# A decoder layer: cross-attention's k and v projected during self-attention and passed through DRAM

## The reference

```python
# self-attention, per batch and head (D = 32)
scores = (q @ k.T + rel_q + rel_k) / sqrt(D)     # rel_q[l, r] = q[l] . dist_emb[l - r + 511]
ctx = softmax(scores) @ v                        # rel_k[l, r] = k[r] . dist_emb[l - r + 511]
x = layernorm(x + layernorm(ctx @ Wo + bo + x))
# cross-attention, per batch and head (64 wide); c is the second input
q, k, v = x @ Wq + bq, c @ Wk + bk, c @ Wv + bv
x = layernorm(x + (softmax(causal(q @ k.T / 8)) @ v) @ Wo + bo)
# slots, 16 experts, and attention from the tokens to the slots
x = layernorm(x + slot_mixture(x))
```

## Time and profile before

| what | value |
|---|---|
| median of 3 runs | 4272.65 us (4272.12 to 4275.99) |
| the profiled execution, its own time | 4274.03 us |
| its span, first to last instruction | 4272.1 us |
| mean granted TensorE clock | 0.942 of full |
| busy share: TensorE, VectorE, ScalarE, POOL | 86%, 52%, 39%, 44% |
| bytes moved by DMA | 1151.74 MB |
| self-attention | about 50 to 1695 us |
| its projection and norms | to about 1945 us |
| cross-attention | about 1945 to 3107 us |

### The profile page before, as it was taken

The page is one execution under the profiler, slowest core; times in us unless marked ns, Lnnn a source line. Parts: engine busy times, 40 slices in busy tenths (PEclk is TensorE's granted clock), DMA queues, the critical chain, the costliest instruction groups (busy, mean ns, idle before and its releaser), DMA issues. The chain is left out here.

```text
span 4272.1 us, 67667 instructions
## 1 busy us (share of the span) xinstructions
PE 3681.4 (86%) x19584; PEld 2298.4 (54%) x19584; DVE 2230.7 (52%) x6128; ACT 1678.6 (39%) x3639; POOL 1859.8 (44%) x1684
## 2 busy tenths in 40 slices
PE   6988888888888886769999999999989987788686
PEld 4766666667676674325556666655545552122244
DVE  4666676767666665773554555455523231111155
ACT  4666666666666664333333333333312110000023
POOL 3766666667676665433444444444511100000012
PEclk9999999999999998989999999999989998898798
DMA  6999999999999997455555555555355328999723
GB/s 246 399 375 391 386 385 374 386 369 386 373 388 377 385 387 295 142 176 194 180 180 175 173 172 176 179 178 180 128 183 186 107 74 350 420 421 421 290 79 118
DMA packets 544321, 1151.74 MB, mean 270 GB/s; under 512 B 34240, under 2 KB 206912, under 8 KB 494912
## 3 DMA queue, kind: packets, MB, share of 16 engines
q1 hardware_dynamic: 539520, 1141.13, 71.7%
q10 hardware_dynamic: 4032, 7.34, 0.5%
q0 software_dynamic: 512, 0.26, 0.0%
HBM read 745.46 MB, written 403.18 MB: 269 GB/s over the span
## 5 line engine op out<-in xcount | busy, mean ns | idle before, releaser
L433 POOL TENSOR_SCALAR a_sc<-a_sc,a_inv 128x512 f32<-128x512 f32 x512 | 818.5, 1602 | 383.1 <-DVE a_inv L383 313.1
L1004 POOL TENSOR_SCALAR b_sc<-b_sc,b_inv 128x128 f32<-128x128 f32 (+3 forms) x512 | 549.6, 1082 | 657.5 <-DVE b_inv L957 657.5
L284 ACT ACTIVATE a_stage_q<-a_ps_q 128x640 f32<-128x640 f32 x512 | 360.0, 703 | 469.8 <-PE a_ps_q L201 442.5
L962 DVE COPY b_pt<-b_ps_t 128x128 f32<-128x128 f32 (+3 forms) x512 | 250.2, 489 | 547.3 <-PE b_ps_t L863 547.3
L390 DVE COPY a_pt<-a_ps_t 128x512 f32<-128x512 f32 x512 | 353.6, 691 | 280.3 <-PE a_ps_t L187 242.3
L376 DVE CUSTOM_DVE_ANT_0 a_sc<-a_ps_s,a_rq 128x512 f32<-128x512 f32 x512 | 353.9, 691 | 197.2 <-PE a_ps_s L177 145.0
L918 ACT ACTIVATE b_sc<-b_sc,b_mx 128x128 f32<-128x128 f32 (+3 forms) x512 | 281.0, 550 | 446.7 <-DVE b_mx L951 446.7
L274 ACT ACTIVATE a_sc<-a_sc,a_mx 128x512 f32<-128x512 f32 x512 | 370.5, 724 | 77.5 <-DVE a_mx L376 75.9
L175 PE MATMUL a_ps_s<-a_ks,a_qs 128*128 128x512 f32 x512 | 261.2, 510 | 139.4 <-DMA a_rk<-band_k 103.9
L284 ACT ACTIVATE a_stage_k<-a_ps_k 128x640 f32<-128x640 f32 x512 | 359.1, 701 | 30.4 <-DMA band_k<-a_stage_k 30.4
L187 PEld LDWEIGHTS a_ps_t<-a_ident,a_sc 128*128 128x128 f32 x2048 | 249.9, 145 | 218.2 <-issue 201.2
(11 more groups left out here) (200 smaller groups left out, 6159.5 us busy)
## 6 DMA issues: line engine op xcount, KB each, us to landing
band_q<-a_stage_q SPq DMA_DIRECT2D x128, 1280.0 KB, 9.0
band_k<-a_stage_k SPq DMA_DIRECT2D x128, 1280.0 KB, 11.6
a_rk<-band_k SPq DMA_DIRECT2D x128, 1024.0 KB, 13.9
a_rq<-band_q SPq DMA_DIRECT2D x256, 512.0 KB, 14.6
d_w<-in_e_W SPq DMA_DIRECT2D x32, 4096.0 KB, 36.9
b_xT<-x1T SPq DMA_DIRECT2D x64, 1024.0 KB, 5.7
b_cT<-in_ctxT SPq DMA_DIRECT2D x64, 1024.0 KB, 8.4
d_wg<-in_e_Wg SPq DMA_DIRECT2D x16, 4096.0 KB, 28.0
```

The lines of the kernel that those rows point to most:

```text
L284: act.activation(st[h % 2][:, t, :].rearrange("p (a n) -> p a n", a=2), src[:, :, 0:WIN // 2], ACT.Copy).then_inc(sem[f"a_{kind}_staged"], 1)
L433: pool.tensor_scalar(sc[n][:, :], sc[n][:, :], inv[:, n:n + 1], None, ALU.mult)\
L1004: pool.tensor_scalar(sc[i][:, 0:width(i)], sc[i][:, 0:width(i)], inv[:, i:i + 1], None, ALU.mult).then_inc(sem["b_normed"], 1)
```

## The change

**In self-attention** each quad also makes k and v of two pairs of cross-attention (project_kv), as the quad's batch is theirs: 16 steps m spread over the 16 tiles by KV_AT, in four groups (k, v, k, v). A group ends in the new PSUM bank ps_o, is evicted by ScalarE into the one buffer kv (kv_out) and stored by SyncE to the DRAM tensors k or v (store_kv). ScalarE issues the loads of the next weights okv, and once a batch of the context oc. To make room, both bands now share three PSUM banks (ps_b), pt holds two heads, and the context is made in two halves, at tiles 11 and 3. Each half uses the four column strips for two heads times two halves of the keys; VectorE moves one strip pair and adds the other (cx_out, two instructions a half). The k projections for later quads move to tiles 13 and 14.

**In cross-attention** TensorE projects q alone. Transposes and context are a whole pair behind the scores, so scores, maxima and sums have two sets of buffers and pt has one. The context has its own bank ps_c and is evicted by ScalarE with v's bias. SyncE loads wq, xT, cols and kT in load, and v apart in load_v. One step of SyncE is load(n+1), store(n-2), load_v(n+1); one of TensorE ends in context(n-1).

```diff
-Q_AT, K_AT, HI_AT = [5, 6, 7, 8], [10, 11, 12, 13], [9, 14]
+Q_AT, K_AT, HI_AT = {5: [0], 6: [1], 7: [2], 8: [3]}, {13: [0, 1], 14: [2, 3]}, [9, 15]
...
+CX_AT, CX_OUT_AT = [HALF + LAG_A, LAG_A], [HALF + LAG_A + 1, LAG_A + 1]
+KV_AT = [[1, 2, 3, 4, 5, 6, 7, 8, 9, 10, 11, 11, 12, 13, 14, 15], list(range(NT)), list(range(NT)),
+         [0, 1, 2, 3, 4, 4, 5, 6, 7, 7, 8, 9, 10, 10, 11, 12]]
...
+            def store_kv(g, n):
+
+                sp.wait_ge(sem["a_kv_out"], 4 * g + n + 1)
+                settle()
+                sp.dma_start(dr[("b_k", "b_v")[n % 2]](2 * g + n // 2), kv[:, :]).then_inc(sem["a_kv_stored"], 16)
+
             def quad(g, j):
                 for h in range(HQ):
+                    if inside(g):
+                        store_kv(g, h)
                     if inside(g + 1):
                         write(g + 1, (j + 1) % 4, h)
...
-            def context(g, j):
-                pe.wait_ge(sem["a_pt_out"], NT * g + NT)
-                if inside(g + 2):
+            def context(g, j, half):
+
+                pe.wait_ge(sem["a_pt_out"], NT * g + HALF * (half + 1))
...
+            def project_kv(g, j, m):
+
+                c, kind, n = m // 8, m // 4 % 2, m % 4
+                if m == 0 and j == 0:
+                    pe.wait_ge(sem["a_oc_in"], 4 * g + 16)
+                if m % 8 == 0:
+                    pe.wait_ge(sem[f"a_okv_in{c}"], 16 * g + 16)
+                if n == 0 and counts(4 * g + m // 4):
+                    pe.wait_ge(sem["a_kv_out"], 4 * g + m // 4)
+                if kind == 0:
+                    mm = pe.matmul(ps_o[:, :], okv[c][:, 0, n, :], oc[:, n, :], start=(n == 0), stop=(n == K4 - 1))
+                else:
+                    for k in range(K4):
+                        mm = pe.matmul(ps_o[:, n * P:(n + 1) * P], oc[:, k, n * P:(n + 1) * P], okv[c][:, 1, k, :],
+                                       start=(k == 0), stop=(k == K4 - 1))
...
+            def kv_out(g, j, n):
+
+                act.wait_ge(sem["a_kv_ready"], 4 * g + n + 1)
+                if counts(4 * g + n):
+                    act.wait_ge(sem["a_kv_stored"], 16 * (4 * g + n))
...
+            def load(n, j):
+
+                if not early(n, 2):
+                    sp.wait_ge(sem["b_q_ready"], n - 1)
                     settle()
-                    sp.wait_ge(sem["b_v_out"], n - 1)
+                    sp.wait_ge(sem["b_score"], NP * (n - 1))
                     settle()
...
+                sp.dma_start(wq[j % 2][:, :, :].rearrange("p k n -> p (k n)"), dr["b_wq"](n)).then_inc(s, 16)
+                sp.dma_start(xT[j % 2][:, :, :], dr["x1T"](n)).then_inc(s, 16)
+                if not early(n, 4):
+                    sp.wait_ge(sem["b_cx_out"], n - 3)
                     settle()
...
+                sp.dma_start(cols[j][:, :], dr["b_cols"](n)).then_inc(s, 16)
+                sp.dma_start(kT[j % 2][:, :], dr["b_k"](n)).then_inc(s, 16)
+
+            def load_v(n, j):
+                if not early(n, 2):
+                    sp.wait_ge(sem["b_cx_ready"], n - 1)
+                    settle()
...
+            def pair(n, j):
+                if inside(n + 1) and not early(n, 1):
+                    load(n + 1, (j + 1) % 4)
+                if not early(n, 2):
+                    store(n - 2, (j - 2) % 4)
+                if inside(n + 1) and not early(n, 1):
+                    load_v(n + 1, (j + 1) % 4)
...
+            def project_q(n, j, k):
+                if k == 0:
+                    pe.wait_ge(sem[f"b_in{j % 2}"], (n - j % 2) * 32 + 64)
```

More of the change, by code:

```diff
@@ L892, in _ @@
-            pe.wait_ge(sem["b_const_in"], 32)
-            for u in range(6):
-                unit(0, 0, u)
-            pe_pair(0, 0, first=True)
-            with pe.Fori(1, PAIRS - 1, 2) as n:
-                pe_pair(n, 1)
-                pe_pair(n + 1, 0)
-            pe_pair(PAIRS - 1, 1, last=True)
-            for i in range(NP - LAG, NP):
-                turn(PAIRS - 1, i)
-            context(PAIRS - 1, 1)
+                    if i in (0, 4) and inside(n):
+                        scores(n, j, i)
@@ L904, in _, with q_out @@
+                    if not early(n, 1):
+                        turn(n - 1, (j - 1) % 4, i)
+                    if i in Q_OF_PAIR and inside(n + 1):
+                        project_q(n + 1, (j + 1) % 4, Q_OF_PAIR.index(i))
+                if not early(n, 1):
+                    context(n - 1, (j - 1) % 4)
+            for k in range(K4):
+                project_q(0, 0, k)
+            pe.wait_ge(sem["b_const_in"], 32)
+            steps(pe, pair)
         @block.scalar
         def _(act):
-            def q_out(n, par):
+            def q_out(n, j):
@@ L937, in _, with pair @@
+            def pair(n, j):
+                for i in range(NP):
+                    if inside(n):
+                        softexp(n, j, i)
+                    if i == 3 and not early(n, 2):
+                        cx_out(n - 2, (j - 2) % 4)
+                if inside(n + 1):
+                    q_out(n + 1, (j + 1) % 4)
+            act.wait_ge(sem["b_in0"], 64)
+            q_out(0, 0)
+            steps(act, pair)
+            cx_out(PAIRS - 1, (PAIRS - 1) % 4)
         @block.vector
         def _(dve):
[L939 to L943 removed]
@@ L987, in _, with pair @@
-            dve.sem_inc(sem["b_cx_out"], 1)
-            dve.wait_ge(sem["b_const_in"], 32)
-            v_out(0, 0)
-            dve_pair(0, 0, first=True)
-            with dve.Fori(1, PAIRS - 1, 2) as n:
-                dve_pair(n, 1)
-                dve_pair(n + 1, 0)
-            dve_pair(PAIRS - 1, 1, last=True)
-            for i in range(NP - LAG, NP):
-                pt_out(PAIRS - 1, 1, i)
-            cx_out(PAIRS - 1, 1)
+            def pair(n, j):
+                for half in (0, 4):
+                    if inside(n):
+                        for i in range(half, half + 4):
+                            add_max(n, j, i)
+                    for i in range(half, half + 4):
+                        if not early(n, 1):
+                            pt_out(n - 1, i)
+                        if inside(n) and i % 2:
+                            invert(n, j, i - 1)
+                            invert(n, j, i)
```

407 lines of the change are left out of this document (201 added, 206 removed).

## The result

The changed kernel takes 4883.56 us (median of 4 runs, 4873.55 to 4886.59) where the kernel before takes 4272.39 beside it (4 runs): a ratio of 1.1426 (95% interval 1.1406 to 1.1445), 611 us slower. The forecast of 4657 had the sign; the time lies above the range of 4440 to 4850. The profiled execution has a span of 4882.5 us at a mean granted clock of 0.898 (before: 4272.1, 0.942).

What follows compares the result with a forecast made beforehand. TensorE's work was taken to bound self-attention, and TensorE plus an exposed late load to set cross-attention's pace. 4274.0 + 313 (self-attention) + 71 (cross-attention) = 4658, so 4657 us for the median; range 4440 to 4850.

Steps and rivals of the forecast that it cites:

- TensorE's work in self-attention: Self-attention: added projections raise TensorE's own work from 41.1 to 55.3 us a quad, the larger bound.
- half clock: Self-attention: 3.4 us of the old quad, taken to go; cross-attention: 1.8 us a pair lost behind the wait.
- The transfers' floor: Self-attention: 21.76 MB a quad at 386 GB/s needs 56.3 us, below TensorE's work with its waits.
- The rule of 358 GB/s a core: Self-attention: the skill's HBM limit would make a quad 60.8 us, total some 25 us higher; set aside for the trace's 378.
- The waits in self-attention: Self-attention, per quad: 2.9 us before contexts, 1.0 before transposes, 0.8 for the kv buffer; the a_rk wait goes.
- Rival 4: Self-attention: the single kv buffer holds up every group, 64 us a quad, total 4786; chance 0.13.
- The late load in cross-attention: Cross-attention: load_v waits for the previous context and delays the loads behind it; TensorE waits 6.4 us a step.
- the transfer's length: Cross-attention: 7.3 us (1.09 + 6.2) from first issue to last landing of the late loads; ends 5.8 and 8.0.
- Nothing behind them: Cross-attention: the late loads, 1,792 KB of v, wq, xT and kT, were assumed to have no transfer queued after them.
- The rest of the pair: Cross-attention, besides the 6.4 us wait: 10.9 us own work, 0.5 for transposes, 1.8 lost clock; pair 19.6 us.
- the clock rule: Cross-attention: the skill says TensorE returns to half rate after gaps; taken as 1.8 us lost in each step.
- Rival 1: Cross-attention: loads not late, pairs of 11.4 us, total 4160, faster than before; decides the sign below 13.1 us; chance 0.12.

Runs made afterwards that it cites:

- e2: Changed kernel with the store of k and v issued by ScalarE on its own queue instead of by SyncE: 4766.2 us.
- e10: Changed kernel with three quarters of the contraction in the k and v projections left out, plus e2's edit: 4631.8 us.
- e7: e2 with the k and v weights loaded once and not again, 1.05 MB a quad less: 4759.9 us against 4766.2.
- e13: The changed kernel measured again, unaltered: 4856.0 us, ratio 1.1369 to the kernel before.
- e8: Changed kernel with SyncE holding the context's store back until the next pair's loads have landed: 4826.5 us.
- e12: e2 with e8's edit added, the context's store held until the loads are in: 4739.1 us.
- e1: Changed kernel with SyncE loading v of pair n in step n instead of v of pair n+1: 4265.8 us, ratio 0.9985 to the kernel before.
- e4: Changed kernel with eight 512-column matmuls on constants ahead of TensorE's wait for the loads in each cross-attention step: 4741.1 us.
- e11: Changed kernel with e1's and e2's edits, plus two transposes and their copies ahead of each score group: 4157.9 us, ratio 0.9732 to the kernel before.

## Why the prediction was right in its sign and wrong in its size

**TensorE's work in self-attention: right.** Own work of 55.3 us a quad was the forecast. Of the 61.5 us measured, TensorE is busy 1830.08/(1990/61.5) = 56.6, part of that at half clock; in e2, at 0.98, it is busy 55.8. e10 and e7 from both sides confirm that it binds.

**The transfers' floor: right within 3%.** 56.3 us were forecast, 54.7 measured (e10). The rule of 358 GB/s a core that the prediction cited from the Trainium skill ("DMA: Bandwidth & Descriptors", Where 436 GB/s comes from) is again not borne out on this one core: 392 GB/s over 1,770 us.

**The waits in self-attention: sum near, parts not.** Forecast 4.7 us a quad (contexts 2.9, transposes 1.0, kv 0.8) at full clock, giving 60.0. Measured in the 32.4 quads of the window: contexts 0.7 (31 waits of 0.7 us, as many as before and half as long, not two a quad of 1.45), transposes 0.3, kv 58.6/32.4 = 1.8, staging 0.5, and 51.8/32.4 = 1.6 that the trace puts down to issue. Of the last, 36.5 us were there before, in six stalls some 250 us apart (before some 200), which is once a batch, in a row of the kernel before that the prediction left out:

```profile
PE a_ps_s L175 <- issue: 35.2, 6, 6.2
```

I had counted them in with half clock, which I took to go; so the 3.4 us a quad that the prediction calls half clock were some 2.3. The other 15.3 us, six stalls of 2.2 to 2.8 us some 5 us behind these, are new; what makes either stall is open. The remaining 56.6 - 55.3 = 1.3 us fit half clock, since the clock is 0.96, and with them that makes 61.5. As 32 x 1.5 = 48 us it is a fifth of the error. Rival 4 was true in a small part: TensorE waits for kv in 19 groups of 128, not in each. Where it waits long is where the prediction expected it, in a batch's last quad; 0.8 us a quad was 1.0 too little.

**The late load in cross-attention: the mechanism right, a term mis-sized.** The wait stands where the prediction put it, in the second tile of each step, ended by kT, 62 times, with the issues right behind the context; the cover is 1.3 us as forecast. The step that failed is "the transfer's length": 7.3 us from the first issue to the last landing, taken from the kernel before between b_wq and b_wk as 1.09 + 6.2. From v's issue to the first q matmul it is, in the mean over 61 steps, 2.6 + 6.7 = 9.4 us in the result's trace and 2.6 + 6.2 = 8.8 in e13's; the range's end was 8.0. What I had wrong for both is the spread of the issues, 2.6 us and not 1.1, as v goes ahead and cols between: I took the distance of three issues for that of the whole burst. The landing itself (6.2) was right for e13 and 0.5 too short for the result. "Nothing behind them" was wrong, since the context's store follows kT by 0.9 us, but that costs 0.5 us a step at most, if anything (e8, e12). The 0.35 us for two semaphores stands on no row; 0.2 us pass between the context's end and v's issue, and the rest is in the 6.7. The wait became 8.2 us a step (e13: 7.7) where 6.4 was forecast.

**The rest of the pair: small, and all on the same side.** Without any late load a pair takes 12.31 us (e1), of which the copies are (51.4 + 9.6)/54 = 1.1: own work of 11.2, not 10.9. In the changed kernel the copies are 47.7/63 = 0.8, not 0.5. What remains of 22.17 is 22.17 - 11.2 - 8.2 - 0.8 = 2.0 for half clock, where 1.8 was forecast; e4, which holds the clock, gains 1.8. With 1.8 from the wait these are the 2.6 us a pair that were missing, over 61 steps some 157 us. The prediction's weighing of the clock rule ("TensorE: Matmul & The Clock Gate" of the Trainium skill, Why this matters for your kernels) stands: in each of the 61 steps the two q instructions behind the wait take 2.07 or 2.08 us where 1.02 is usual.

**The error in sum.** 4883.6 - 4657 = 227 us: 157 from the pair, 48 from the quad, and 22 from the first steps and the stretch between the stages, where forecast and spans cut the time in different places. In e13 the same kernel stands 6 us above the range, and 28 of the 227 would not be there: 33 less in the pairs (63 x 0.53) and 5 more ahead of them. The range held no case in which both stages come out near their upper ends; the quad, 61.5, lay inside its ends of 57 and 64, and the pair at 22.17 just above its end of 22.0.

**Rival 1**, the loads not late, was made by e1: 4266, not 4160. The pair came to 12.31 us, not 11.4, and the quad to (2055.8 - 114.0)/31.5 = 61.6, not 60.0. Its condition for the sign, a pair below 13.1 us, was met, but with the 361 us that self-attention really lost that limit is 17.97 - 361/64 = 12.3, just where the pair came out. So mending the load alone brings the change to no gain worth the name; with e2's edit too it is 2.3% faster, and 2.7% with e11's.

## What to carry to other kernels

In an in-order queue look at which load waits for the latest consumer, and at what stands behind it: a load placed "early" for the next pair held four others back and cost 9 us a step, and one moved line gave 590 us back. A single buffer between an engine and a store comes free only as early as the store's queue lets it. When sizing a late transfer, count from the first issue of its burst to the last landing with all that is issued right behind it, and leave in the sum those stalls of before that the change doesn't touch.

## What the runs showed of the hardware

- One program measured twice: kT landed after 7.1 us in the median once and 5.8 the other time (two groups of steps near 5.5 and 7.3 us, in other shares), and the kernel took 4883.6 and 4856.0 us, while the kernel before took 4272.4 and 4272.5. Where a transfer's length is on the critical path, compare kernels that ran together.
- A store of 256 KB took 11 us from issue to landing on SyncE's queue, behind the bands, and 6.6 on ScalarE's own, with the same transfers a quad (e2).
- After rests of 6.6 to 9.4 us the two instructions behind took 2.07 or 2.08 us, twice their usual time, in each of 61 steps of the changed kernel, with a granted clock of 0.50 in the window read. In e4 they were slow behind six rests of 1.97 to 2.22 us and fast behind the 44 others, one of 2.34 us among them. Work on constants during the wait gave 115 us net.
- The stage moved 392 GB/s over 1,770 us (e10), more than the 378 of the kernel before.
